# The second-pass mask of a first attention, taken from TensorE to GpSimd and VectorE

## What is computed

```python
scores = jnp.einsum('bhqd,bhkd->bhqk', qp, kp)
scores = jnp.where(pad_mask == 0, -jnp.inf, scores)
scores = jnp.where(attn_mask == 0, -jnp.inf, scores)
attn = jax.nn.softmax(scores / sqrt(HD), axis=-1)
out = jnp.einsum('bhqk,bhkd->bhqd', attn, vp).reshape(-1, seq, D)
```

## Time and profile before

| | us |
|---|---|
| runs: median (lowest to highest) | 3132.17 (3118.64 to 3132.75) |
| the profiled execution | 3123.59 |
| its span | 3121.8 |
| TensorE matmuls busy | 2919.3 (94%) |
| VectorE busy | 1675.5 (54%) |
| ScalarE busy | 1288.4 (41%) |
| GpSimd busy | 561.0 (18%) |
| L469 and L486, 512 matmuls each | 20.3 to 512.2 and 45.5 to 537.1 |

### The profile page before, as it was taken

How to read it: one execution, slowest core, us unless ns; L and a number is a source line. 1 busy time by engine, 2 the same in 40 slices (tenths; PEclk the granted TensorE clock), 3 DMA queues, 4 the chain that set the end, 5 groups by cost and what they waited for, 6 DMA issues and landing times.

```text
span 3121.8 us, 66485 instructions
## 1 busy us (share of the span) xinstructions
PE 2919.3 (94%) x27840; PEld 2035.1 (65%) x27840; DVE 1675.5 (54%) x3245; ACT 1288.4 (41%) x1809; POOL 561.0 (18%) x518
## 2 busy tenths in 40 slices
PE   7999999999999999999889889899999999999998
PEld 5666666677777776666656556566566666666666
DVE  5666665544444445555667776665555544444331
ACT  1333333444444433444444444344444544444443
POOL 0111111122222212111123333320111110000000
PEclk9999999999999999999999998899999999999999
DMA  2201000100000001000011010001000000000000
GB/s 87 86 28 33 23 22 23 42 23 22 22 22 22 22 16 37 25 25 29 26 37 39 23 33 24 17 19 62 22 22 29 30 28 29 28 27 24 21 25 11
DMA packets 77927, 92.48 MB, mean 30 GB/s; under 512 B 14361, under 2 KB 59561, under 8 KB 77634
## 3 DMA queue, kind: packets, MB, share of 16 engines
q1 hardware_dynamic: 77634, 88.23, 8.9%
HBM read 39.67 MB, written 4.19 MB: 14 GB/s over the span
## 4 chain that ended last, share of the span: by engine, by line
PE 85%; DVE 8%; ACT 3%; issue 2%; DMA 1%; SPq 1%; DVEq 0%; ACTq 0%
PE ps_nat L465 24%; PE ps_misc L555 9%; PE ps_pv L625 9%; PE ps_misc L684 9%; PE ps_misc L706 7%; PE ps_misc L580 5%; DVE mx L912 4%; PE ps_misc L657 4%; PE ps_misc L636 2%; PE ps_nat L469 2%; ACT pt L763 2%; PE ps_misc L674 2%; PE ps_st L486 2%; PE ps_misc L550 2%; PE ps_st L482 2%
## 5 line engine op out<-in xcount | busy, mean ns | idle before, releaser
L912 DVE TENSOR_REDUCE mx<-ps_nat 128x4 f32<-128x1024 f32 x640 | 782.5, 1223 | 791.9 <-PE ps_nat L465 675.4
L763 ACT ACTIVATE pt<-ps_st 128x1024 f32<-128x1024 f32 (+1 forms) x768 | 758.7, 988 | 1082.8 <-PE ps_st L482 596.6
L465 PE MATMUL ps_nat<-k,q 17*128 17x256 f32 (+1 forms) x6144 | 867.7, 400 | 120.6 <-DVE mx L912 84.1
L482 PE MATMUL ps_st<-q,k 18*128 18x256 f32 (+1 forms) x6144 | 867.7, 401 | 0.1
L465 PEld LDWEIGHTS ps_nat<-k,q 17*128 17x128 f32 x6144 | 522.2, 189 | 364.7 <-issue 176.0
L482 PEld LDWEIGHTS ps_st<-q,k 18*128 18x128 f32 x6144 | 516.5, 189 | 2.8 <-issue 1.7
L625 PE MATMUL ps_pv<-pt,vaug 128*32 128x256 f32 (+1 forms) x6144 | 416.2, 390 | 0.0
L1038 POOL TENSOR_TENSOR rstd<-var,half_pow 128x2 f32<-128x2 f32 x144 | 101.7, 706 | 1368.8 <-DVE var L814 1368.5
L684 PE MATMUL ps_misc<-xF,weights 128*128 128x256 f32 x1152 | 287.2, 394 | 17.8 <-ACT xF L777 17.8
L1046 POOL TENSOR_TENSOR xn<-xn,tiles 128x512 f32<-128x512 f32 x128 | 163.8, 1280 | 667.5 <-DVE xn L818 667.5
L625 PEld LDWEIGHTS ps_pv<-pt,vaug 128*32 128x32 f32 x6144 | 164.0, 111 | 181.4 <-issue 111.7
(11 more groups left out here) (104 smaller groups left out, 3141.1 us busy)
## 6 DMA issues: line engine op xcount, KB each, us to landing
q<-plain SPq DMA_DIRECT2D x320, 64.0 KB, 2.6
k<-plain SPq DMA_DIRECT2D x320, 64.0 KB, 2.5
weights<-in_weights SPq DMA_DIRECT2D x19, 512.0 KB, 4.0
cT<-in_ctx_t SPq DMA_DIRECT2D x32, 256.0 KB, 2.7
cn<-in_ctx SPq DMA_DIRECT2D x32, 256.0 KB, 3.0
xT<-in_x_t SPq DMA_DIRECT2D x16, 256.0 KB, 3.3
xn<-in_x SPq DMA_DIRECT2D x16, 256.0 KB, 2.9
out<-xn SPq DMA_DIRECT2D x16, 256.0 KB, 2.0
```

The costliest lines, as they stand in the source:

```text
L465: return nc.tensor.matmul(ps_nat[:, j, hf, 0:keys], lhs, rhs, start=hf == 0, stop=last)
L482: return nc.tensor.matmul(ps_st[:, j, kh, 0:S - q0], lhs, rhs, start=kh == first, stop=last)
L763: nc.scalar.activation(pt[:, g % PT_SLOTS, :, 0:used], ps_st[:].rearrange("p j a b -> p j (a b)")[:, :, 0:used], ACT.Exp, scale=SCALE).the ...
L912: last = nc.vector.reduce_max(out, ps_nat[:], AX)
```

## The change

The second-pass mask of the first attention leaves TensorE. The exponentials are taken from unmasked second-pass scores, and `pt` is then masked in place. For six pairs GpSimd multiplies the bits of `pt`, read as int32, with `keep_bits`, 0 or 1. For pairs 2 and 5 (`BY_DVE`) VectorE takes the minimum of `pt` and `keep_cap`, which is 0 or 1e30. Each is one instruction on 128 partitions and 1024 elements. The weighted sums wait for these (`kept_pool`, `kept_dve`) instead of for the exponentials, and the sums and their copies are planned one step later in the first attention. The bias "pb" on GpSimd moves from 20.15 to 3.5. `st_done` is raised behind the scores. The first-pass masks stay. VectorE makes one more constant at the start.

```diff
+BY_DVE = (2, 5)
...
-    0: [("otr", 0, 13.8), ("otr", 1, 17.1), ("ott", 0, 18.8), ("opr", 0, 19.1), ("pb", 0, 20.15),
+    0: [("otr", 0, 13.8), ("otr", 1, 17.1), ("ott", 0, 18.8), ("opr", 0, 19.1), ("pb", 0, 3.5),
...
             add(8 * n + p + LAG, "st", n, p, 1)
+            if a == 0:
+                add(8 * n + p + LAG + (0.9 if p in BY_DVE else 0.1), "keep", n, p)
+        late = 1 if a == 0 else 0
         for i in range(2):
             add(8 * n + 4 * i + 4.6, "nmt", n, i)
-            add(8 * n + 4 * i + LAG + 4.4, "pvout", n, i)
+            add(8 * n + 4 * i + LAG + 4.4 + late, "pvout", n, i)
         for c in range(QUADS):
-            add(8 * n + 2 * c + LAG + 2, "pvg", n, c, 2)
+            add(8 * n + 2 * c + LAG + 2 + late, "pvg", n, c, 2)
...
-                    last = kh != first and attention(n) not in (0, 2)
+                    last = kh != first and attention(n) != 2
...
-                    if attention(e[1]) == 0:
-                        return nc.tensor.matmul(ps_st[:, j, kh, :], ident_b[:], mask0_t[:, kh, :], start=False, stop=kh == 1)
...
-                            if st and attention(st[1]) not in (0, 2):
+                            if st and attention(st[1]) != 2:
                                 last_st.then_inc(st_done, 1)
...
-                    if st and attention(st[1]) in (0, 2):
+                    if st and attention(st[1]) == 2:
...
-                        pe.wait_ge(exp_done, nth(("st", n, 2 * i + 1)))
+                        if a == 0:
+                            pe.wait_ge(kept_pool, nth(("keep", n, 2 * i + 1), lambda m, j: j not in BY_DVE))
+                            pe.wait_ge(kept_dve, nth(("keep", n, 2 * i + 1), lambda m, j: j in BY_DVE))
+                        else:
+                            pe.wait_ge(exp_done, nth(("st", n, 2 * i + 1)))
...
-                for dst, src in ((mask0, xn[:, B - 1]), (mask0_t, xn[:, B - 2])):
+                for dst, src, op, by in ((mask0, xn[:, B - 1], ALU.is_equal, NEG), (keep_bits, xn[:, B - 2], ALU.not_equal, 1.0),
+                                         (keep_cap, xn[:, B - 2], ALU.not_equal, -NEG)):
...
+                    if kind == "keep" and i in BY_DVE:
+                        dve.wait_ge(exp_done, nth(("st", n, i)))
+                        part = pt[:, (n * PAIRS + i) % PT_SLOTS].rearrange("p j (a b) -> p j a b", a=2)
+                        keep = keep_cap[:].unsqueeze(1).to_broadcast([P, 2, 2, S])
+                        nc.vector.tensor_tensor(part, part, keep, ALU.min).then_inc(kept_dve, 1)
...
+                    if kind == "keep" and i not in BY_DVE:
+                        pool.wait_ge(exp_done, nth(("st", n, i)))
...
+                        part = pt[:, (n * PAIRS + i) % PT_SLOTS].rearrange("p j (a b) -> p j a b", a=2).bitcast(I32)
+                        keep = keep_bits[:].unsqueeze(1).to_broadcast([P, 2, 2, S])
+                        nc.gpsimd.tensor_tensor(part, part, keep, ALU.mult).then_inc(kept_pool, 1)
```

More of the change, by code:

```diff
@@ L202, in block_kernel @@
         mask0 = sb("mask0", [P, 2, S], BF16)
-        mask0_t = sb("mask0_t", [P, 2, S], BF16)
+        keep_bits = sb("keep_bits", [P, 2, S], I32)
+        keep_cap = sb("keep_cap", [P, 2, S])
         causal = sb("causal", [P, P], BF16)
@@ L275, in block_kernel @@
         nat_done, max_done = sem("nat_done"), sem("max_done")
+        kept_pool, kept_dve = sem("kept_pool"), sem("kept_dve")
         st_done, exp_done, pv_done, ote_ready = sem("st_done"), sem("exp_done"), sem("pv_done"), sem("ote_ready")
@@ L381, in _ @@
                         if u == B - 3:
-                            sp.wait_ge(const_made, 4)
+                            sp.wait_ge(const_made, 5)
                         sp.dma_start(xn[:, u], t["x"][u]).then_inc(x_loaded[u], 16)
@@ L436, in need_nat @@
                         if n == 0:
-                            pe.wait_ge(const_made, 5)
+                            pe.wait_ge(const_made, 6)
                         if attention(n) == 0:
@@ L833, in _ @@
                 dve.wait_ge(raw_masks, 48)
-                for dst, src in ((mask0, xn[:, B - 1]), (mask0_t, xn[:, B - 2])):
+                for dst, src, op, by in ((mask0, xn[:, B - 1], ALU.is_equal, NEG), (keep_bits, xn[:, B - 2], ALU.not_equal, 1.0),
+                                         (keep_cap, xn[:, B - 2], ALU.not_equal, -NEG)):
                     nc.vector.tensor_scalar(dst[:].rearrange("p a b -> p (a b)"), src.rearrange("p a b -> p (a b)").bitcast(I32),
-                                            0.0, NEG, ALU.is_equal, ALU.mult).then_inc(const_made, 1)
+                                            0.0, by, op, ALU.mult).then_inc(const_made, 1)
                 for c, dst in enumerate((causal, causal_t)):
@@ L844, in _ @@
                     x = xn[:, u]
-                    if kind == "pad":
+                    if kind == "keep" and i in BY_DVE:
[3 more added lines that the diff above has]
+                        nc.vector.tensor_tensor(part, part, keep, ALU.min).then_inc(kept_dve, 1)
+                    elif kind == "pad":
                         dve.wait_ge(pad_loaded, 16)
@@ L1014, in _ @@
                     x = xn[:, u]
-                    if kind == "pb":
+                    if kind == "keep" and i not in BY_DVE:
+                        pool.wait_ge(exp_done, nth(("st", n, i)))
+                        if n == 0 and i == 0:
+                            pool.wait_ge(const_made, 3)
+                        part = pt[:, (n * PAIRS + i) % PT_SLOTS].rearrange("p j (a b) -> p j a b", a=2).bitcast(I32)
+                        keep = keep_bits[:].unsqueeze(1).to_broadcast([P, 2, 2, S])
+                        nc.gpsimd.tensor_tensor(part, part, keep, ALU.mult).then_inc(kept_pool, 1)
+                    elif kind == "pb":
                         if u == 0 and i == 0 and a <= 1:
```

## The result

| | before | after |
|---|---|---|
| median of six runs each (lowest to highest) | 3132.46 (3118.64 to 3134.73) | 3154.29 (3149.72 to 3164.44) |
| the profiled execution | 3123.59 | 3149.72 |
| its span | 3121.8 | 3147.9 |
| TensorE matmuls busy | 2919.3 | 2898.2 |
| VectorE busy | 1675.5 | 1736.8 |

The medians are 22 us apart. The ratio is 1.0085, with a 95% interval from 1.0059 to 1.0112: slower by 0.85%. The forecast was 3145, the range 3108 to 3176. So the time lies in the range, but the forecast that the change stays within 0.5% (15.7 us) did not hold.

A forecast was written before the change was run, and what follows sets the result against it. TensorE work bounds some score steps, the chain through exponentials or maximum the others. Steps sum to 31.23 against 31.24 us per element, so 0, plus 13 us of lower clock on 3132.2: 3145, range 3108 to 3176.

The forecast's parts named there:

- The removed matmuls and the floor: Second-pass mask matmuls off TensorE: 3.44 us per element, but the maximum's chain keeps every score step at 3.00 or more.
- S1, S5 and S7: Second, sixth and eighth of an element's eight score steps; forecast 3.37, 3.44 and 3.00 us, waiting for the maximum.
- Rival (1): First attention: the floor isn't one and all 3.44 us per element go, 3077 (0.07), or part, 3108 to 3116 (0.13).
- The moved sums: Weighted-sum groups one step later each in the first attention: 1.21 us leaves one step and enters the next.
- S0, S2, S4 and S6: First, third, fifth and seventh score steps, which receive the sums; forecast 4.70, 4.35, 4.03 and 3.92 us.
- The minima: Two VectorE minima per element at 1.22 us each, one hidden, the other making the next maximum 0.43 us late.
- The products: Six GpSimd integer products per element at 2.54 us each, GpSimd at 19.4 of 31.2 us, ready before the weighted sums.
- (3): Integer product costs 5.08 us on GpSimd and the weighted sums wait for it: 3188 us, chance 0.08.
- (4): A VectorE minimum is caught behind a GpSimd product, the next maximum 2.5 us late: 3172 us, chance 0.08.
- The lock: VectorE instructions with two SBUF inputs wait for GpSimd instructions to end; layer norm's small steps delayed, hidden by 0.3 us.
- The clock: TensorE idle stretches of 1.2 to 1.4 us, 30 in the stage, one in three lowering the clock: 13 us.
- rival (2): Clock falls after nearly each TensorE idle stretch, 20 to 30 falls: 26 to 51 us, 3158 to 3183, chance 0.17.

The follow-up runs named there:

- e12: The changed kernel once more, nothing edited: median 3165.20, ratio 1.0115 to the kernel before.
- e3: The kernel before without the first attention's second-pass mask matmuls, nothing in their place, sums where they were: median 3086.02, ratio 0.9869.
- e11: The changed kernel with only the first weighted sum late and one transpose of the values moved a step earlier: median 3097.93, ratio 0.9901.
- e4: The kernel before with only the first attention's weighted sums and copies one step later, masks still on TensorE: median 3159.25, ratio 1.0099.
- e7: The changed kernel with each GpSimd product done twice in a row: median 3245.99, ratio 1.0374 to the kernel before.
- e5: The changed kernel with the weighted sums back in their earlier steps, masks still on GpSimd and VectorE: median 3156.51, ratio 1.0092 to the kernel before.
- e1: The changed kernel with eight useless matmuls behind the scores of each element's last step in the first attention: median 3126.65, ratio 1.0007 to the kernel before.
- e9: The changed kernel with the sixth step's four small transposes done three times, filling that wait instead: median 3153.35, ratio 1.0080 to the kernel before.
- e6: The changed kernel with all eight pairs masked on GpSimd and no minimum on VectorE: median 3127.90, ratio 1.0000 to the kernel before.

## Why the prediction was right, point by point

The time fell into the range, and the working of the steps holds. The number owes something to luck: the steps gave 5 us more than forecast, the clock in the stage took 9 us more, and another 8 us that the prediction had at nothing were lost behind the stage. A second execution of the same program (e12) lost 41 us to the clock, and one of its runs (3179.56) lies outside the range.

- **The removed matmuls and the floor: right.** S1, S5 and S7 end with the maximum. TensorE is idle there for 0.63, 1.07 and 1.51 us, where the prediction had 0.93, 1.40 and 1.58 less 0.2 each. e3 measured 2.96 of the 3.44 us, with two steps at 3.00 and 3.01. Rival (1), that the saving arrives, fell; e3 and e11 show that it was there to be had, by another placing of the rest.
- **The moved sums: right.** S0, S2, S4 and S6 are within 0.11 of the forecast, S3 within 0.05. e4 gives their price by itself.
- **The minima: right in price, a little too dear in place.** The end of VectorE's work that the prediction puts at 5.35 behind the start of S1 adds up to 5.29 by its own terms; it was 5.14, so that minimum delayed nothing. In S5 the instructions in front overlap: the maximum starts 1.93 into the step (193.22), not 2.16, and the step is 3.19 instead of 3.44. In S7 I was too cheap: the next scores start 0.22 after the maximum's end instead of 0.05, and the step is 3.17. Together the sum is 30.90 instead of 31.23, 5 us less in the stage.
- **The products: right.** 2.35 against 2.54, and 0.2 us of waits where they are. Rivals (3) and (4) fell: of the 32 minima the longest took 1.42 us. e7 shows both mechanisms when a product costs twice as much, and e5 a sum that does wait for its product.
- **The lock: right**, and stronger than the row of before: also the smallest steps of the layer norm wait for the product's end. They lie in S0's cover. L818 (now L826) wasn't doubled, though I had expected that: in the rows above it starts behind the product's end and takes 0.74 us, as before.
- **The clock: the term that was too small.** I had 10 falls of 1.3 us among 30 idle stretches, in S5 and S7 alike. It was none in S5 and up to every one in S7; a fall mostly lasts 6.8 us instead of 3.4 and costs 3.2. That is 22 us in the first profile and 41 in the second, where I had 13, partly offset by the 5 us of the steps. The price per 3.4 us of low clock was 1.6, near the 1.7 that I had named as the most. The mechanism of rival (2) therefore acts, from a different set of stretches; the median lies between the forecast (3145) and that rival (3158 to 3183), outside the 0.5%. The Trainium skill, "TensorE: Matmul & The Clock Gate", section "Why this matters for your kernels", warns of idle gaps far longer only; the runs here speak against taking 1.5 us as harmless, since e1 and e9 differ in which gap they leave and by 0.73%, 23 us.
- **What I didn't foresee: the 8.1 us behind the stage.** The window from 540 to 660 has a clock of 0.90 against 0.99: behind a wait of 0.97 us at 551.36 it is low for 13.7 us, and twice more later. e1 has the same (95.9 us between the two maxima, against 86.9 before), e3 hasn't (86.9). With the late sums but no products (e4) they are 91.1 apart, with the products but early sums (e5) 94.4; e9 and e12 have 92.0 and 92.3. So each of the two without the other, crossing into the second attention, goes with a part of it. No run was made that changes this stretch alone, and its cause stays open.

What stays open beside that: which moments are harmless, and so why e6 was spared, in its trace and, to judge by the times, in all ten runs.

## What to carry to other kernels

Work taken from the engine that bounds is worth only what the chain behind it leaves; list what ends next-latest in each step first, and move other work into the steps that begin to wait, or the gain shows up as idle time. Such idle time isn't free even where the sum of the steps is unchanged: stretches of 1.5 us in a TensorE that is otherwise busy cost the clock here, and a few useless matmuls in them were worth 24 us. When a moved operation must be late for one consumer, make it late for that one alone: one late sum instead of four was worth about 42 us, half of it in the steps (1.35 us in each of 16 elements) and the rest, about 20 us, near the 22 that the clock took in the stage.

## What the runs showed of the hardware

- The same idle stretch of 1.5 us lowered the clock in none, in 8 or in 13 elements of three executions (e6, after, e12), of which the last two are of one program; the stretches of 1.07 us in S5 (after, e1) weren't followed by a low clock once, those of 1.2 us in e4 neither, those of 2.17 us in 8 of 12 cases (e5). Single ones of 0.97 us (after, 551.36), 1.21 us (before, 538.57) and 1.32 us (e3, 442.31) were.
- An int32 product of 128x1024 on GpSimd takes 2.35 us, 1.85 times the float sum of 128x512 (1269 ns); a float minimum of 128x1024 on VectorE 1.20.
- VectorE instructions from SBUF to SBUF of two elements per partition wait for a GpSimd product to end: L986 took 1.82 us instead of 0.16, L822 0.57 instead of 0.17 (195.41 to 195.98, beside a product that ended at 195.95). The batch statistics and what reads PSUM beside such a product kept their times (the maximum 1.23).
